# Attention opening of a four-stage kernel: another order of the prologue and of the row maxima, and weights issued by ScalarE

## What is computed

```
q = Wq @ norm(x) + bq;  k = Wk @ ctx + bk;  v = Wv @ ctx + bv      # per batch, 128 channels x 256 positions
q, k = rotary(q), rotary(k)
scores = einsum("bdhn,bdhm->bhnm", q, k) / sqrt(8)
out = Wm @ (softmax(scores) @ v) + bm;   x = x + out
```

## Time and profile before

| | |
|---|---|
| median of 3 runs | 474.33 us (473.31 to 475.53) |
| profiled execution | 475.81 us |
| its span | 474.0 us |
| busy in the span | PE 375.1, DVE 325.5, ACT 175.3, POOL 64.5 us |
| mean granted clock of TensorE | 0.903 of full speed |
| chain that ended last | PE 51%, DVE 32%, issue 7%, DMA 5%, ACT 3%, POOL 2% |

### The profile page before, as it was taken

How to read it: one execution, slowest core, us unless ns; L and a number is a source line. 1 busy time by engine, 2 the same in 40 slices (tenths; PEclk the granted TensorE clock), 3 DMA queues, 4 the chain that set the end, 5 groups by cost and what they waited for, 6 DMA issues and landing times.

```text
span 474.0 us, 7584 instructions
## 1 busy us (share of the span) xinstructions
PE 375.1 (79%) x2754; PEld 222.0 (47%) x2754; DVE 325.5 (69%) x893; ACT 175.3 (37%) x237; POOL 64.5 (14%) x151
## 2 busy tenths in 40 slices
PE   5257677378877867999999999999869777486895
PEld 4113233233333324466666667666545445354363
DVE  8875578479888647285545537586785877868785
ACT  1104446155565641143343333433453434432001
POOL 0323424244342200000000000000000000000000
PEclk9755889899999976999999999999995978977899
DMA  7551642626655120000000000225025454540011
GB/s 241 149 173 58 182 132 72 198 70 203 193 188 175 66 78 0 1 0 0 2 0 0 1 0 0 76 82 143 14 72 163 129 147 127 168 136 1 1 46 44
DMA packets 61971, 41.81 MB, mean 88 GB/s; under 512 B 3952, under 2 KB 59760, under 8 KB 61936
## 3 DMA queue, kind: packets, MB, share of 16 engines
q1 hardware_dynamic: 61360, 41.10, 28.6%
q10 hardware_dynamic: 576, 0.23, 0.2%
HBM read 26.71 MB, written 14.42 MB: 87 GB/s over the span
## 4 chain that ended last, share of the span: by engine, by line
PE 51%; DVE 32%; issue 7%; DMA 5%; ACT 3%; POOL 2%; DVEq 0%; POOLq 0%
PE psum L627 13%; PE psum L640 13%; DVE mx L1169 6%; DMA qstk<-mT 5%; PE psum L534 4%; PE psum L715 4%; PE psum L615 3%; PE psum L498 2%; PE psum L519 2%; DVE stats L1144 2%; ACT prob L880 2%; DVE rope_ab L1158 2%; DVE rs_a L1133 1%; DVE rs_a L1132 1%; PE psum L483 1%
## 5 line engine op out<-in xcount | busy, mean ns | idle before, releaser
L1169 DVE TENSOR_REDUCE mx<-psum 128x2 f32<-128x512 f32 x128 | 81.1, 683 | 25.4 <-PE psum L498 24.5
L880 ACT ACTIVATE prob<-psum 128x1024 f32<-128x1024 f32 x64 | 64.1, 1022 | 73.7 <-PE psum L519 73.6
L1381 DVE SCALAR_TENSOR_TENSOR xall<-psum,comb,xall 128x256 f32<-128x256 f32 x128 | 53.1, 477 | 41.5 <-PE psum L640 41.1
L627 PE MATMUL psum<-xnT,wup 128*128 128x512 f32 x160 | 76.2, 600 | 0.0
L640 PE MATMUL psum<-wdn,act 128*128 128x256 f32 x320 | 75.5, 379 | 0.6 <-DVE xall L1378 0.6
L640 PEld LDWEIGHTS psum<-wdn,act 128*128 128x128 f32 x320 | 60.7, 190 | 25.9 <-issue 19.1
L929 ACT ACTIVATE rel<-psum 128x512 f32<-128x512 f32 x40 | 23.9, 597 | 97.3 <-PE psum L627 97.3
L330 POOL TENSOR_TENSOR parts<-qk_rest,parts 128x512 bf16<-128x512 f32 x15 | 17.3, 1156 | 229.9 <-ACT parts L955 225.0
L534 PE MATMUL psum<-prob,vt 128*32 128x256 f32 x512 | 39.1, 424 | 6.4 <-ACT prob L880 5.8
L985 ACT ACTIVATE prob<-psum 128x1024 f32<-128x1024 f32 x32 | 32.6, 1024 | 25.8 <-PE psum L737 25.8
L627 PEld LDWEIGHTS psum<-xnT,wup 128*128 128x128 f32 x160 | 30.2, 194 | 22.7 <-issue 21.0
(11 more groups left out here) (153 smaller groups left out, 470.8 us busy)
## 6 DMA issues: line engine op xcount, KB each, us to landing
qstk<-stack_scratch SPq DMA_DIRECT2D x32, 256.0 KB, 3.7
kstk<-stack_scratch SPq DMA_DIRECT2D x32, 256.0 KB, 4.4
stack_scratch<-parts SPq DMA_DIRECT2D x32, 192.0 KB, 2.1
stack_scratch<-parts SPq DMA_DIRECT2D x32, 128.0 KB, 2.1
wup<-in_wup SPq DMA_DIRECT2D x4, 640.0 KB, 6.4
wdn<-in_wdn SPq DMA_DIRECT2D x4, 640.0 KB, 8.0
stack_scratch<-parts SPq DMA_DIRECT2D x32, 64.0 KB, 1.8
out<-xall SPq DMA_DIRECT2D x8, 128.0 KB, 1.7
```

The source lines that it names most:

```text
L627: last = nc.tensor.matmul(psum[:, n % 2, :], wup[:, f, BLOCKS[g], :], xnT[:, f, c * HALF:(c + 1) * HALF], start=(f == 0), stop=(f == 1))
L880: nc.scalar.activation(prob[(b * PAIRS + k) % 3][:], exp_buf(k).rearrange("p a n -> p (a n)"), ACT.Exp, scale=SCALE).then_inc(exp_done, 1)
L1169: nc.vector.tensor_reduce(mx[:, half, :, 4 * s + p4:4 * s + p4 + 1], bank.rearrange("n (b m) -> n b m", b=2), AX_X, ALU.max).then_inc(misc ...
L1381: last = nc.vector.scalar_tensor_tensor(out=xall[:, b, :], in0=src, scalar=comb[:, b, e:e + 1], in1=xall[:, b, :], op0=ALU.mult, op1=ALU.add)
```

## The change

- Prologue: the maxima of batch 0 come in earlier: pairs 0 to 2 ahead of k of batch 2, pair 3 ahead of its q, the others behind. TensorE waits for `eye_in` before k of batch 0, not before the maxima. VectorE's second portion of statistics stands behind q of batch 1.
- Maxima in the steps: `MAXES` and `MAXT` now run 10 pairs ahead from batch 1 on: batch 0 takes 10 pairs, batches 1 to 5 take 8, batch 6 takes 6. Transposes at spots 2, 8 and 14 in batch 0, 6 and 14 after.
- GpSimd: `vt[1]`'s memset moves here from VectorE. In the prologue normalize(3) comes ahead of rotate of batch 2, and the negation of batch 0's first half between `rest(2)` and `third(2)`, the second behind `third(2)`. In the steps, the negation of half 0 stands ahead of `rotate`, that of half 1 behind `third`.
- SP: batch 0's parts are written in seven transfers, by part, each as soon as it is there (`first_to_dram`); the reads of kstk of batch 0 are issued by ScalarE; parts of batch 2 are written ahead of the second rows of batch 0.
- ScalarE issues ctx[2], ctx[3:], and the experts' weights (after the second exp of batches 1 to 4), and does batch 2's parts before its first exp.

```diff
-        MAXES = {0: [[(1, k)] for k in range(8)],
-                 1: [[(2, k)] for k in range(6)] + [[(2, 6), (3, 0)], [(2, 7), (3, 1)]],
-                 2: [[(3, k + 2)] for k in range(5)] + [[(3, 7), (4, 0)], [(4, 1)], [(4, 2), (4, 3)]],
-                 6: [[(7, k + 4)] if k < 4 else [] for k in range(8)],
+        MAXES = {0: [[(1, 0), (1, 1)], [(1, 2), (1, 3)], [(1, 4)], [(1, 5)], [(1, 6)], [(1, 7)], [(2, 0)], [(2, 1)]],
+                 6: [[(7, k + 2)] if k < 6 else [] for k in range(8)],
                  7: [[]] * 8}
-        MAXES.update({b: [[(b + 1, k + 4) if k < 4 else (b + 2, k - 4)] for k in range(8)] for b in (3, 4, 5)})
-        MAXT = {0: {4: (0, 1), 10: (1, 0)}, 1: {2: (1, 1), 10: (2, 0)}, 2: {2: (2, 1), 6: (3, 0), 14: (3, 1)}, 7: {}}
-        MAXT.update({b: {4: (b + 1, 0), 12: (b + 1, 1)} for b in (3, 4, 5, 6)})
+        MAXES.update({b: [[(b + 1, k + 2) if k < 6 else (b + 2, k - 6)] for k in range(8)] for b in range(1, 6)})
+        MAXT = {0: {2: (0, 1), 8: (1, 0), 14: (1, 1)}, 7: {}}
+        MAXT.update({b: {6: (b + 1, 0), 14: (b + 1, 1)} for b in range(1, 7)})
...
-        PROLOGUE = [("cb", 0), ("k", 0), ("q", 0), ("v", 0), ("k", 1), ("q", 1), ("k", 2), ("q", 2)]
+        PROLOGUE = ([("cb", 0), ("k", 0), ("q", 0), ("v", 0), ("k", 1), ("q", 1)]
+                    + [("max", 0, n) for n in range(3)] + [("k", 2), ("max", 0, 3), ("q", 2)]
+                    + [("max", 0, 4), ("max", 0, 5), ("maxT", 0, 0), ("max", 0, 6), ("max", 0, 7)])
         FIRST = 2
-
-        FIRST_MAX = list(range(6)) + [None] + list(range(6, PAIRS))
-        N_PRO = len(PROLOGUE) + 2 * PAIRS + 1
+        PRO_AT, N_PRO = {}, 0
+        for use_ in PROLOGUE:
+            PRO_AT[use_] = N_PRO
+            N_PRO += banks_of(use_)
...
+        def parts_count(b):
+            return 96 * (b // SETS + 1) + 16 * (b % SETS == 0)
...
+            def first_to_dram():
+
+                src = parts[0]
+                sp.wait_ge(hi_done, 1)
+                sp.dma_start(by_channel(0, 0, 0, 3), src[:, 0, 0:1, :].broadcast_to((P, 3, D))).then_inc(parts_out[0], 16)
+                sp.dma_start(by_channel(0, 1, 0, 4)[:, 0:4:3, :], src[:, 1, 0:1, :].broadcast_to((P, 2, D))
+                             ).then_inc(parts_out[0], 16)
+                sp.dma_start(by_channel(0, 1, 5, 1), src[:, 1, 0:1, :]).then_inc(parts_out[0], 16)
+                sp.wait_ge(mid_done, 1)
+                sp.dma_start(by_channel(0, 0, 3, 2), src[:, 0, 1:2, :].broadcast_to((P, 2, D))).then_inc(parts_out[0], 16)
+                sp.dma_start(by_channel(0, 1, 1, 4)[:, 0:4:3, :], src[:, 1, 1:2, :].broadcast_to((P, 2, D))
+                             ).then_inc(parts_out[0], 16)
+                sp.wait_ge(lo_done, 1)
+                sp.dma_start(by_channel(0, 0, 5, 1), src[:, 0, 2:3, :]).then_inc(parts_out[0], 16)
+                sp.dma_start(by_channel(0, 1, 2, 1), src[:, 1, 2:3, :]).then_inc(parts_out[0], 16)
...
-            def inner_weights(first):
-
-                e = bass.ds(first, CHUNK)
-                sp.dma_start(wup[:, :, e, :], t["wup"][:, :, e, :]).then_inc(ffn_in, 16)
-                sp.dma_start(wdn[:, e, :], t["wdn"][:, e, :]).then_inc(ffn_in, 16)
-
-            sp.wait_ge(fill_out, 16 * 2 * SETS)
-            for b in range(2):
-                parts_to_dram(b)
-                for half in range(2):
-                    stack_from_dram(b, half)
-            max_rows(0, 0, len(PROLOGUE) + 2 * FIRST_MAX.index(None) + 1)
-            sp.dma_start(ctx_all[:, 3:NB, :], t["ctx"].rearrange("b p d -> p b d")[:, 3:NB, :]).then_inc(ctx_rest, 16)
-
             def rows_at(b, half):
                 max_rows(b, half, A_AT["maxT", b, half] + 1)
 
+            sp.wait_ge(fill_out, 16 * 2 * SETS)
+            first_to_dram()
+            sp.wait_ge(parts_out[0], parts_count(0))
+            for half in range(2):
+                sp.dma_start(qstk[0][:, 4 * half:4 * half + 4, :], stack_rows(0, 0, half)).then_inc(stack_in[0][half], 16)
+            parts_to_dram(1)
+            for half in range(2):
+                stack_from_dram(1, half)
+            max_rows(0, 0, PRO_AT["maxT", 0, 0] + 1)
+            parts_to_dram(2)
             rows_at(0, 1)
-            parts_to_dram(2)
             for half in range(2):
                 stack_from_dram(2, half)
-            rows_at(1, 0)
-            parts_to_dram(3)
-            for half in range(2):
-                stack_from_dram(3, half)
-            for b in (1, 2):
-                rows_at(b, 1)
-                rows_at(b + 1, 0)
-                parts_to_dram(b + 3)
-                if b == 2:
-                    rows_at(3, 1)
-                for half in range(2):
-                    stack_from_dram(b + 3, half)
-                inner_weights(CHUNK * (b - 1))
-            for b in (3, 4):
+            for b in range(5):
                 rows_at(b + 1, 0)
                 parts_to_dram(b + 3)
                 rows_at(b + 1, 1)
                 for half in range(2):
                     stack_from_dram(b + 3, half)
...
+            pe.wait_ge(eye_in, 32)
+            for use in PROLOGUE[1:]:
+                kind, b = use[0:2]
+                u = PRO_AT[use]
+                if u + banks_of(use) > 3:
+                    pe.wait_ge(misc_free, u - 3 + banks_of(use))
...
+            act.dma_start(ctx_all[:, 2, :], t["ctx"][2]).then_inc(ctx_in[2], 16)
             act.drain().then_inc(exp_done, 1)
-            for b in range(2):
-                first_parts(b)
-                second_parts(b)
+
+            def inner_weights(first):
+
+                e = slice(first, first + CHUNK)
+                act.dma_start(wup[:, :, e, :], t["wup"][:, :, e, :]).then_inc(ffn_in, 16)
+                act.dma_start(wdn[:, e, :], t["wdn"][:, e, :]).then_inc(ffn_in, 16)
+
+            first_parts(0)
+            second_parts(0)
+            act.wait_ge(parts_out[0], parts_count(0))
+            for half in range(2):
+                act.dma_start(kstk[0][:, 4 * half:4 * half + 4, :], stack_rows(0, 1, half)).then_inc(stack_in[0][half], 16)
+            first_parts(1)
+            second_parts(1)
+            act.dma_start(ctx_all[:, 3:NB, :], t["ctx"].rearrange("b p d -> p b d")[:, 3:NB, :]).then_inc(ctx_rest, 16)
+            first_parts(2)
+            second_parts(2)
 
             for b in range(NB):
                 for k in range(PAIRS):
                     exps(b, k)
-                    if b == 0 and k == 0:
-                        first_parts(2)
-                    if b == 0 and k == 1:
-                        second_parts(2)
+                    if 1 <= b <= 4 and k == 1:
+                        inner_weights(CHUNK * (b - 1))
...
+            nc.gpsimd.memset(vt[1][:], 0.0).then_inc(init, 1)
+            pool.wait_ge(init, 2)
+            ones_of(nc.gpsimd, 1)
...
+            rotate(PRO_AT["q", 1] + 1)
+            rest(1, 1)
+            third(1, 1)
             pool.wait_ge(stats_ready, 1)
-            pool.wait_ge(misc_free, PROLOGUE.index(("q", 1)) + 1)
             normalize(3)
+            rotate(PRO_AT["q", 2] + 1)
             rest(2, 0)
+            negate(PRO_AT["max", 0, 3] + 2, 0)
             third(2, 0)
+            negate(PRO_AT["max", 0, 7] + 2, 1)
             for b in range(NB):
                 if b:
                     divide(b - 1)
+                if b + 1 < NB:
+                    negate_at(b + 1, 0)
                 if b + 3 < NB:
                     rotate(A_AT["k", b + 3] + 1)
-                if b in (0, 1):
-                    negate_at(b + 1, 0)
-                elif b == 2:
-                    negate_at(3, 0)
-                elif b + 1 < NB:
-                    negate_at(b + 1, 1)
-                if b + 3 < NB:
                     rest(b + 3, (b + 3) % 2)
                     if b + 4 < NB:
-                        pool.wait_ge(misc_free, PROLOGUE.index(("q", 2)) + 1 if b == 0 else A_AT["q", b + 2] + 1)
+                        pool.wait_ge(misc_free, PRO_AT["q", 2] + 1 if b == 0 else A_AT["q", b + 2] + 1)
                         normalize(b + 4)
                     third(b + 3, (b + 3) % 2)
...
+                    if (kind, b) == ("q", 1):
+                        dve.wait_ge(x_in[1], 16)
+                        norm_stats(FIRST, NB - FIRST)
+                        normalize(2, 0)
+                        nc.vector.tensor_scalar(nmean[:], mv[:, :, 0], -1.0, None, ALU.mult).then_inc(stats_ready, 1)
```

More of the change, by code:

```diff
@@ L320, in y_banks, with stack_rows, ones_of @@
             return psum[:, 2:4, :] if y % 2 == 0 else psum[:, 6:8, :]
+        def stack_rows(par, ten, half):
+            return scr[par, ten].rearrange("(k r) n -> r k n", r=P)[:, 4 * half:4 * half + 4, :]
+        def parts_count(b):
+            return 96 * (b // SETS + 1) + 16 * (b % SETS == 0)
+        def ones_of(eng, par):
+            halves = vt[par][:].rearrange("m a (g t j) r -> m (a g) t j r", g=2, t=2)
+            eng.memset(halves[:, :, 0, :, 24:25], 1.0)
```

(31 more changed lines are left out.)

59 lines of the change are left out of this document (14 added, 45 removed).

## The result

| | before | after |
|---|---|---|
| median of 4 runs each | 474.86 us (473.31 to 475.53) | 462.07 us (461.4 to 462.9) |
| ratio | | 0.974, 95% interval 0.971 to 0.977 |
| profiled execution, its span | 475.81, 474.0 us | 462.08, 460.3 us |
| mean granted clock of TensorE | 0.903 | 0.915 |
| chain that ended last: DMA, POOL | 5%, 2% | 2%, 4% |

The forecast was 464.2 us, range 458 to 471.

The account below looks back on a forecast made before the run. VectorE's row maxima pace batches 3 and 4; batches 0 to 2 stall, TensorE waiting for rows. 41.2 + 19.8 + 16.0 + 3 x 15.7 + 2 x 14.1 = 152.3 against 162.4: 474.3 - 10.1 = 464.2 us, range 458 to 471.

Parts of the forecast that it names:

- Rows' waits go: TensorE's waits for row maxima (3.7 us in batch 0, 9.0 in batches 1 and 2) vanish, rows being issued earlier.
- Opening: Up to the first exp: eye wait costs 0.9 us, negation comes later; first exp 41.2 instead of 37.2, 4.0 us lost.
- 23.9 + 8.6: Opening on VectorE: maxes start at 23.9, then three pairs, k2, pair 3 and q2; q2 taken at 32.5 us.
- Negation: Opening, GpSimd: rotate and rest of batch 2 precede batch 0's first negation; 4.9 us, ending at 37.4 instead of 33.2.
- Stacks of batch 0: Opening: seven piecewise writes bring the first stack read up to 2 us sooner, covered by VectorE's statistics; gain 0.
- Batch 0: First attention: 22.0 us less 5.8 of waits plus 2.8 for two more pairs is 19.0; 19.8 taken, bounds 17.7 and 21.8.
- Batches 1 to 4: Attention loop: pv waits 0.3 us for the second half's negation behind third; batch 1 16.0 us, the others 15.7 each.
- Weights: Issued on ScalarE's queue in batches 1 to 4: cost 0, bounds 3 us for late rows and 4.8 for the issues.
- Batches 5, 6: Last forecast attention batches: 14.1 us each; batch 5 from 14.5, batch 6 from 12.3 with six pairs, losing 1.8.
- A: Rival: weights beside stack reads land late, TensorE stops at max(b+2,0), 1.5 us in four batches; 470 us, chance 0.13.
- C: Rival: GpSimd's negations become the bound, deciding from a period of 17.7 us; 477 us at 18.2; chance 0.07.
- B: Rival: more gained, with upper clock from the first exp, opening costing 2.5, batch 6 keeping 12.3; 459 us, chance 0.12.

Follow-up runs that it names:

- e1: Changed kernel with the experts' weights issued by SP again, behind the four stack reads of batches 1 to 4; median 462.1 us, ratio to before 0.987.
- e2: Kernel before the change with only the weights' issues moved to ScalarE, behind the third exp of batches 2 to 5; 476.1 us, ratio 1.018.
- e0: The changed kernel run again without an edit; median 462.2 us, ratio to before 0.975.
- e5: Changed kernel with each turn's four transposes of the maxes one step later, behind a pv instead of in front; 457.9 us, ratio to before 0.969.
- e6: Changed kernel with the eye matrix awaited before the first maxima, e4's earlier negation and e5's later transposes together; 453.2 us, ratio to before 0.952.
- e10: e6 with the weights issued one exp later, after the third exp of batches 1 to 4; 451.4 us, ratio to before 0.946.
- e4: Changed kernel with GpSimd negating batch 0's first half ahead of rotate and rest of batch 2; 460.6 us, ratio to before 0.981.
- e9: e6 with batch 0's parts written in six transfers behind the last part, not piecewise in seven; 454.4 us, ratio to before 0.956.

## Why the prediction was right, step by step

| | forecast | measured |
|---|---|---|
| opening, first exp | 41.2 | 42.4 |
| batch 0 | 19.8 | 18.7 |
| batch 1 | 16.0 | 15.4 |
| batches 2 to 4, each | 15.7 | 15.2 |
| batches 5 and 6, each | 14.1 | 14.0 |
| end of batch 6 | 152.3 | 150.1 |

- **Rows' waits go.** Right: 14.6 us became 0.5. The cause was right as well: issued earlier, not from another queue (e1, e2). The rule of the Trainium skill, "DMA: Bandwidth & Descriptors", section "Issuing engines are not separate DMA queues", was borne out: e2's rows took 6.3 us beside weights on another queue, and e1 lost nothing. What I drew from the same page's section "Queues, rings and completion order", that the rows would land well before the weights since the queues take turns, the traces contradict: in e2 wdn landed at 88.8 and TensorE had the rows at 89.92, and it took 5.6 to 6.4 us for 12 KB issued 0.5 to 1.8 us behind wup, with wdn ahead of it or 0.1 us behind (e0, e5, e6), against at most 4.4 in front of it (e10). That is against what I drew and not against the taking of turns itself: SP's own writes or reads stood ahead of the rows on their queue each time. The sum did not use it.
- **Opening.** The mechanism was right (first the eye matrix, then GpSimd's negation behind rotate and rest), and the size 1.2 us short, in one term: "eye16 lands 4.4 us later, at 6.57". k got it at 7.83, so k moved 2.1 us instead of 0.9. I took one execution's landing time for a fixed one. The landing of eye16 (32 KB) in e2, whose opening is that of before:

```profile
eye<-in_eye ACTq DMA_DIRECT2D x1, 32.0 KB, 5.7
```

  and in e1, whose opening is the changed one, with ctx[2] behind it on ScalarE's queue:

```profile
eye<-in_eye ACTq DMA_DIRECT2D x1, 32.0 KB, 4.6
```

  It was 4.4 before the change, 5.6 in the changed kernel and 6.3 in e10. So ctx[2] isn't needed for a late landing, and what sets it is not shown. The sum of what stands behind has two slips that cancel: "23.9 + 8.6" adds up to 8.8 by its own terms (8.9 measured), and "it was 4.0 us" less the 0.4 of mT gives 3.6 (measured) where 3.8 was added.
- **Negation.** "4.9 us, so the negation ends at 37.4": it ended at 38.8; 1.2 of the 1.4 is the eye's delay, 0.2 the first of those slips. Removing the order's cost gave 2.8 (e4), since TensorE then has the other maxima and q of batch 2 ahead of the transposes.
- **Stacks of batch 0.** Gain 0 held: VectorE got to the maxima at 25.14, 1.4 us after the stacks were in. With the statistics no longer in front (e6, e9) the piecewise writes are worth 0.5.
- **Batch 0.** 18.7, within the bounds of 17.7 and 21.8; the clock was 0.73, as before. The 5.8 us of waits that were to go went (the 0.5 us for rows is ahead of the first exp), and a wait of 1.0 for `mpart` at its end was new; the 1.1 us below the value taken is not broken down. The upper bound doesn't follow from its terms: 15.2 us at 0.73 is 22.3 at the lower level before the two pairs, not 21.8 with them.
- **Batches 1 to 4.** The named wait was there (the transposes at spot 14 for `mpart`, 0.7 us in each batch) and e5 shows that it was on the path: 15.2 with it, 14.6 without. "15.5 + 0.3" was taken from batch 4, and the period came 0.5 us below that; which link of the loop was shorter was not separated.
- **Weights.** Cost 0, right in that run, for a narrower reason than the one given: the rows of half 1, which I took for safe since they are used at spot 6 of the next batch, left only 0.2 to 0.5 us ahead of wup. I had reckoned the half-0 rows, 8 us later, which never waited in batches 1 to 4. My range also left out the bound of 4.8 us for the weights' issues on ScalarE; none of it came: the periods are 15.2 without them too (e1).
- **Batches 5, 6.** 14.0 each; the loss of 1.7 in batch 6 was as forecast.
- **Rivals.** A did not come in the change, but it is what met e5 and e6, at another place (rows instead of stacks). C was off by far: the transposes' wait stayed at 0.7. The total lay between the forecast and B.
